# Short attention of a gated cross-attention block: row maxima as the bias of single exponentials, and a third buffer for context rows

## The reference, cut to what matters

```python
scores = einsum('bhqd,bhkd->bhqk', qh, kh) * inv_sqrt_d     # inv_sqrt_d = 1/sqrt(16)
scores = where(causal, scores, finfo(float32).min)
attn   = softmax(scores, axis=-1)
out    = einsum('bhqk,bhkd->bhqd', attn, vh)
# layers 1 to 3, ahead of their own attention over 1500 context rows of width 64:
kv_rope = kv_c * cos + rotate_half(kv_c) * sin
```

## Time and profile before

| | us |
|---|---|
| median of 3 runs | 2336.41 |
| lowest and highest run | 2328.46, 2338.89 |
| the profiled execution, own time | 2332.07 |
| its span, first to last instruction | 2330.3 |
| PE busy in the span | 2184.0 (94%) |
| DVE, ACT, POOL busy | 1478.2, 924.0, 1095.6 |
| mean granted TensorE clock | 0.963 |

### The profile page before, as it was taken

One profiled execution on the slowest core, in us unless ns is written; L12 is line 12 of the kernel. 1 busy time (PEld: TensorE's weight loads), 2 busy tenths in 40 slices (PEclk: granted clock), 3 DMA queues, 4 the chain that ended last, 5 costly groups with the idle time before them and its releaser, 6 DMA issues. The chain is left out here.

```text
span 2330.3 us, 38656 instructions
## 1 busy us (share of the span) xinstructions
PE 2184.0 (94%) x13766; PEld 1556.0 (67%) x13766; DVE 1478.2 (63%) x2519; ACT 924.0 (40%) x1433; POOL 1095.6 (47%) x618
## 2 busy tenths in 40 slices
PE   6768999999999998999999999897999999998998
PEld 4447998666566657666655665797665665677997
DVE  2765444577777757787777775412777777744444
ACT  1442443434444442113444444112444444424443
POOL 0330332047777760564777777101177777722332
PEclk9878999999999999999999999899999999998999
DMA  4482732374555513226455461384845545304332
GB/s 83 130 256 82 225 117 81 108 182 100 132 122 112 127 30 127 60 79 148 104 123 131 103 135 31 110 336 188 240 106 131 110 113 133 74 6 118 113 114 83
DMA packets 122054, 285.59 MB, mean 123 GB/s; under 512 B 31355, under 2 KB 73903, under 8 KB 118172
## 3 DMA queue, kind: packets, MB, share of 16 engines
q1 hardware_dynamic: 121244, 281.95, 45.6%
q0 software_dynamic: 672, 1.84, 0.2%
HBM read 237.15 MB, written 46.41 MB: 122 GB/s over the span
## 5 line engine op out<-in xcount | busy, mean ns | idle before, releaser
L1275 DVE TENSOR_REDUCE keep_top<-banks 128x1 f32<-128x500 f32 x945 | 596.0, 675 | 218.4 <-PE banks L1182 218.3
L1352 ACT ACTIVATE att_ex<-banks 125x896 f32<-125x896 f32 x576 | 500.9, 918 | 231.7 <-PE banks L1175 231.5
L1208 PE MATMUL banks<-att_ex,att_v 125*64 125x448 f32 x2304 | 464.7, 545 | 0.0
L1407 POOL TENSOR_TENSOR att_acc<-att_acc,att_ex 125x896 f32<-125x896 f32 x186 | 391.9, 2107 | 67.3 <-ACT att_ex L1352 53.5
L1407 POOL TENSOR_TENSOR att_acc<-att_acc,att_two 125x896 f32<-125x896 f32 x141 | 297.6, 2110 | 165.0 <-DVE att_two L1291 165.0
L1182 PE MATMUL banks<-keep_kh,keep_qt 64*128 64x500 f32 x1230 | 369.4, 406 | 2.8 <-POOL keep_eye L1390 2.8
L1208 PEld LDWEIGHTS banks<-att_ex,att_v 125*64 125x64 f32 x2304 | 152.5, 136 | 247.9 <-issue 209.3
L1175 PE MATMUL banks<-keep_qt,keep_kh 64*125 64x448 f32 x1152 | 308.8, 403 | 7.9 <-ACT att_ex L1352 2.7
L1175 PE MATMUL banks<-keep_qt,att_kl 64*125 64x448 f32 x1152 | 307.2, 363 | 0.0
L1722 PE MATMUL banks<-moe_xs,moe_w 128*128 128x448 f32 x1272 | 283.9, 373 | 4.0 <-DVE moe_w L1818 2.4
L1291 DVE TENSOR_TENSOR att_two<-att_ex 125x896 f32<-125x896 f32 x144 | 244.4, 1697 | 62.2 <-ACT att_ex L1352 59.5
(11 more groups left out here) (274 smaller groups left out, 2687.5 us busy)
## 6 DMA issues: line engine op xcount, KB each, us to landing
keep_kh<-kvt_hi SPq DMA_DIRECT2D x96, 375.0 KB, 5.2
att_kl<-kvt_lo SPq DMA_DIRECT2D x96, 375.0 KB, 7.2
q_rows<-mats_q SPq DMA_DIRECT2D x24, 896.0 KB, 4.8
keep_qt<-q_rows SPq DMA_DIRECT2D x96, 224.0 KB, 6.0
moe_raw<-L_experts_dram SPq DMA_DIRECT2D x53, 384.0 KB, 4.3
att_v<-kvn SPq DMA_DIRECT2D x24, 720.0 KB
sort_wu<-L_experts_dram SPq DMA_DIRECT2D x14, 1024.0 KB, 9.9
moe_cb<-comb_rows SPq DMA_DIRECT2D x62, 224.0 KB
```

Of the source, the lines that this page charges most:

```text
L1208: last = pe.matmul(PS[WEIGHED][64 * e:64 * e + 64, 0:HALF], v[:, s // 2, u, s % 2, :], ex[:, u % RING, e, :], start=u == 0, stop=u == UNIT ...
L1275: dve.tensor_reduce(top[:, s % 2, n // NS, n % NS:n % NS + 1], PS[MAXIMA + n % 3][:, 0:SB], AX.X, ALU.max).then_inc(mx_done, 1)
L1352: act.activation(ex[:, u % RING], scored, ACT.Exp).then_inc(exp_done, 1)
L1407: pool.tensor_tensor(a, a if n else ex[:, 0], two[:, i] if k == 2 else ex[:, k], ALU.add).then_inc(gathered, 1)
```

## The change

`Rotation` gets a third buffer of `cn`, loaded ahead like the first two (SP loads three pairs in an earlier stage, and pair m+1 instead of pair m in turn m of this stage), and a second buffer of `cm`, a tile of its own. POOL takes the sines of pair m+1 ahead of the sums of pair m; their wait is on the sums of pair m-1. DVE takes the cosines ahead of the two lows.

In `attend_short` DVE no longer subtracts the maxima from 448 or 336 columns; it multiplies the maxima with -SCALE into a small tile `nmx` (8 or 6 columns). DVE no longer sums the rows. ACT takes one exponential per tile of 128 rows and batch, 56 columns each, 14 for each pair, with `nmx` as the bias and `accum_out` for the sum of the row into `rs`. The semaphore `exp_done` goes up at the last of 8 and at the last of 6. DVE's inverses wait on it.

```diff
--- before.py
+++ after.py
@@ -180,14 +180,15 @@
     def __init__(self, G, keep):
         self.G = G
         self.cosN, self.sinN = keep.sb("cosN", [KP, NC * D]), keep.sb("sinN", [KP, NC * D])
-        self.cn = keep.sb("cn", [KP, 2, 2, NC * D])
-        self.cm = G["xn"][0:KP].rearrange("p t h -> p (t h)")[:, 0:2 * NC * D].rearrange("p (b n) -> p b n", b=2)
+        self.cn = keep.sb("cn", [KP, 3, 2, NC * D])
+        early = G["xn"][0:KP].rearrange("p t h -> p (t h)")[:, 0:2 * NC * D].rearrange("p (b n) -> p b n", b=2)
+        self.cm = [early, keep.sb("cm", [KP, 2, NC * D])]
         self.out_n, self.out_t = G["kvn_out"], G["kvt_out"]
 
     def start(self, st):
         self.cr = st.sb("cr", [KP, NC, 2, D])
         self.hi, self.lo = st.sb("hi", [128, 2, L], F32R), st.sb("lo", [128, 2, L], F32R)
-        self.in_n = [st.sem(f"in_n{u}") for u in range(2)]
+        self.in_n = [st.sem(f"in_n{u}") for u in range(3)]
         self.sin_n, self.cos_n, self.sum_n, self.turned, self.hi_t, self.lo_t = (
             st.sem(n) for n in ("sin_n", "cos_n", "sum_n", "turned", "hi_t", "lo_t"))
 
@@ -196,7 +197,7 @@
         for dst, src in ((self.cosN, "cosN"), (self.sinN, "sinN")):
             for a, z in self.ROWS:
                 yield dst[a:z, :], self.G[src][a:z, :]
-        for m in range(2):
+        for m in range(3):
             for a, z in self.ROWS:
                 yield self.cn[a:z, m], self.pair(m, a, z)
 
@@ -204,9 +205,9 @@
         return self.G["ctxN"][2 * m:2 * m + 2, a:z].rearrange("b p n -> p b n")
 
     def load(self, sp, m):
-        sp.wait_ge(self.sum_n, 2 * m - 2)
+        sp.wait_ge(self.sum_n, 2 * m - 4)
         for a, z in self.ROWS:
-            sp.dma_start(self.cn[a:z, m % 2], self.pair(m, a, z)).then_inc(self.in_n[m % 2], 16)
+            sp.dma_start(self.cn[a:z, m % 3], self.pair(m, a, z)).then_inc(self.in_n[m % 3], 16)
 
     def store_values(self, sp, m):
         sp.wait_ge(self.sum_n, 2 * m + 2)
@@ -220,17 +221,17 @@
         sp.dma_start(self.G["kvt_lo"][rows, :], self.lo[:, u, :].bitcast(FP32)).then_inc(self.out_t[u], 16)
 
     def sines(self, pool, m):
+        if m >= 3:
+            pool.wait_ge(self.in_n[m % 3], m // 3 * 32)
         if m >= 2:
-            pool.wait_ge(self.in_n[m % 2], m // 2 * 32)
-        if m:
-            pool.wait_ge(self.sum_n, 2 * m)
-        pool.tensor_tensor(self.cm[:], self.cn[:, m % 2],
+            pool.wait_ge(self.sum_n, 2 * m - 2)
+        pool.tensor_tensor(self.cm[m % 2][:, :, :], self.cn[:, m % 3],
                            self.sinN[:, :].unsqueeze(1).broadcast_to([KP, 2, NC * D]),
                            ALU.mult).then_inc(self.sin_n, 1)
 
     def cosines(self, dve, m):
         dve.wait_ge(self.sin_n, m + 1)
-        dve.tensor_tensor(self.cn[:, m % 2], self.cn[:, m % 2],
+        dve.tensor_tensor(self.cn[:, m % 3], self.cn[:, m % 3],
                           self.cosN[:, :].unsqueeze(1).broadcast_to([KP, 2, NC * D]), ALU.mult).then_inc(self.cos_n, 1)
 
     def sums(self, eng, m, e):
@@ -239,7 +240,7 @@
         if m:
             eng.wait_ge(self.turned, 3 * m)
             eng.wait_ge(self.out_n, 32 * m)
-        cn, cm = (v.rearrange("p b (c e d) -> p c b e d", e=2, d=D // 2) for v in (self.cn[:, m % 2], self.cm[:]))
+        cn, cm = (v.rearrange("p b (c e d) -> p c b e d", e=2, d=D // 2) for v in (self.cn[:, m % 3], self.cm[m % 2]))
         cr = self.cr[:].rearrange("p c b (e d) -> p c b e d", e=2)
         eng.tensor_tensor(cr[:, :, :, e], cn[:, :, :, e], cm[:, :, :, 1 - e], ALU.add).then_inc(self.sum_n, 1)
 
@@ -848,11 +849,10 @@
     GROUPS = ((0, 4), (4, NT))
     with Stage(nc, "att0") as st:
         p, pT = st.sb("p", [128, NT, 2, 64]), st.sb("pT", [128, T])
-        mx, rs = st.sb("mx", [128, NT, 2]), st.sb("rs", [128, NT, 2])
+        mx, nmx, rs = st.sb("mx", [128, NT, 2]), st.sb("nmx", [128, NT, 2]), st.sb("rs", [128, NT, 2])
         rot.start(st)
-        padded, s_ready, masked, maxed, centred, exp_done, summed, inverted, scaled = (
-            st.sem(n) for n in ("padded", "s_ready", "masked", "maxed", "centred", "exp_done", "summed", "inverted",
-                                "scaled"))
+        padded, s_ready, masked, maxed, negated, exp_done, inverted, scaled = (
+            st.sem(n) for n in ("padded", "s_ready", "masked", "maxed", "negated", "exp_done", "inverted", "scaled"))
         t_ready, t_copied, o_ready, placed = (st.sem(n) for n in ("t_ready", "t_copied", "o_ready", "placed"))
 
         def scored(m, g):
@@ -870,8 +870,8 @@
             def _(sp):
                 Stage.semaphores.clear_earlier(sp)
                 for m in range(B // 2):
-                    if m >= 2:
-                        rot.load(sp, m)
+                    if 3 <= m + 1 <= LAST:
+                        rot.load(sp, m + 1)
                     if m:
                         rot.store_values(sp, m - 1)
                     if m >= 2:
@@ -938,21 +938,18 @@
                     for g, (a, z) in enumerate(GROUPS):
                         dve.wait_ge(masked, 2 * m + g + 1)
                         dve.tensor_reduce(mx[:, a:z, :], scored(m, g), AX.X, ALU.max).then_inc(maxed, 1)
-                    for g in range(2):
+                    for g, (a, z) in enumerate(GROUPS):
                         dve.wait_ge(maxed, 2 * m + g + 1)
-                        dve.tensor_tensor(scored(m, g), scored(m, g), of_rows(mx, g), ALU.subtract).then_inc(centred, 1)
+                        dve.tensor_scalar(nmx[:, a:z, :], mx[:, a:z, :], -SCALE, None, ALU.mult).then_inc(negated, 1)
+                    rot.cosines(dve, m)
                     if m:
                         rot.turned_lows(dve, m - 1, 0)
                         rot.turned_lows(dve, m - 1, 1)
-                    rot.cosines(dve, m)
                     if m == LAST:
                         rot.turned_lows(dve, m - 1, 2)
                         rot.sums(dve, m, 0)
                     for g, (a, z) in enumerate(GROUPS):
                         dve.wait_ge(exp_done, 2 * m + g + 1)
-                        dve.tensor_reduce(rs[:, a:z, :], scored(m, g), AX.X, ALU.add).then_inc(summed, 1)
-                    for g, (a, z) in enumerate(GROUPS):
-                        dve.wait_ge(summed, 2 * m + g + 1)
                         dve.reciprocal(rs[:, a:z, :], rs[:, a:z, :]).then_inc(inverted, 1)
                     if m:
                         dve.wait_ge(t_ready, 2 * m)
@@ -985,9 +982,14 @@
                     if m:
                         rot.turned_highs(act, m - 1, 0)
                         rot.turned_highs(act, m - 1, 1)
-                    for g in range(2):
-                        act.wait_ge(centred, 2 * m + g + 1)
-                        act.activation(scored(m, g), scored(m, g), ACT.Exp, scale=SCALE).then_inc(exp_done, 1)
+                    for g, (a, z) in enumerate(GROUPS):
+                        act.wait_ge(negated, 2 * m + g + 1)
+                        for t in range(a, z):
+                            for u in range(2):
+                                row = scored(m, g)[:, t - a, u, :]
+                                last = act.activation(row, row, ACT.Exp, bias=nmx[:, t, u:u + 1], scale=SCALE,
+                                                      accum_out=rs[:, t, u:u + 1])
+                        last.then_inc(exp_done, 1)
                     if m:
                         place(m - 1)
                         rot.turned_highs(act, m - 1, 2)
@@ -1005,8 +1007,10 @@
             def _(pool):
                 pool.memset(p[:, :, :, S:], 0.0).then_inc(padded, 1)
                 pool.wait_ge(G["ahead_in"], G["ahead_expected"])
+                rot.sines(pool, 0)
                 for m in range(B // 2):
-                    rot.sines(pool, m)
+                    if m < LAST:
+                        rot.sines(pool, m + 1)
                     rot.sums(pool, m, 1)
 
 
```

## The result

The changed kernel takes 2354.79 us (median of 6 runs, 2346.44 to 2360.05), the kernel before 2333.37 us in runs taken beside them (6 runs, 2327.93 to 2338.89). The ratio is 1.0093, its 95% interval 1.0075 to 1.011: slower by 21.7 us, 17.5 to 25.7. The profiled execution took 2360.05 us, 28.0 more than the one of before; it is the slowest of the six, so its span overstates the loss.

A forecast was written before the change was run, and what follows sets the result against it. A loop through ACT, DVE and PE was taken to set the stage's pace. Six rounds +12.7, start +1.3 and end +3.8 gave 112 t - 19.2, +17.8 us at 330 ns: 2350 us, range 2329 to 2364.

The forecast's parts named there:

- ring: In short attention: highs, exponentials, place, highs, `pT` on ACT, then PE, then highs again; 11.39 us each time before.
- t: Time from one new exponential to the next on ACT; bounded at 127 to 420 ns, taken as 330.
- three signs of being wrong: Exponentials starting less than 276 ns apart; `pT` still waiting for PE in each pair; time moving in another stage.
- The round: One turn of the ring: 8.88 + 14 t, 13.50 us at 330 ns; six rounds 81.0 instead of 68.33, +12.7.
- ACT becomes gapless from first highs to `pT`, and DVE is hidden: Per pair, ACT's 1.51 us idle ahead of `pT` goes; about 2.0 us through DVE and PE hides behind ACT's work.
- Start: Pair 0, up to `pT`: 14 t - 3.34, +1.3 us at 330 ns.
- End: Pair 7, first to third highs: 14 t - 0.79, +3.8 us at 330 ns.
- The gain of cosines sooner: With sines a pair ahead, DVE's cosines stop waiting for POOL (once 1.21 us); already counted in the new round.
- the higher price: Rival: sum and exponential don't overlap on ACT, t 420 ns, +27.8 us, 2360 us; chance 0.15.
- the cheap sum: Rival: t near 217 ns, +5.1 us, 2337 us; chance 0.29 together with full clock in all six `weigh`.
- faster: Rival: exponentials at 127 ns and full clock in every `weigh`, -15.7 us, 2316 us; chance 0.08.
- The contention: Rival: DVE's cosines slowed beside POOL's sines, 9.4 us over eight pairs, 2359 us if on the path; chance 0.04.

The follow-up runs named there:

- place_split: The changed kernel with two of the four copies of `place` moved from ACT to DVE, behind the lows; one profile only, 2348.93 us.
- soft_only: The kernel before with only the softmax part of the change; ratio 1.007 (1.0053 to 1.0087) to the kernel before.
- third_late: The changed kernel with the third pair's two loads issued one stage later, in the fold stage; ratio 1.0094 (1.0059 to 1.013).
- rot_only: The kernel before with only the rotation part: three buffers, three loads ahead, sines a pair ahead, cosines ahead of the lows; ratio 1.0017 (0.9994 to 1.004).
- before_all_later: The kernel before with context rows, tables and next weights all issued one stage later, in the fold stage; ratio 0.998 (0.997 to 0.999).

## Why the prediction was right, and where it was not

The forecast was +17.8 us against a measured 21.7 (17.5 to 25.7), by the mechanism it named: the new exponentials lengthen a ring through ACT and PE. That the number came so near is luck in part, since errors of several us stood against one another. With the measured t its sum gives +12.5, so 5.3 us of the forecast were a t taken too long. Against that it had at nothing the wait of the transposes for `place` (4.8 us in six rounds), a slower PE in the first rounds (1.6), the barrier behind the third load (3.9) and 1.1 us at the start of the stage; with these and the -0.2 above, 12.5 comes to the 23.7 us by which the stage ends later in the profile.

Two of the prediction's three signs of being wrong were met. `pT` still waits for PE in each pair, if only for 5.9 us in eight waits instead of 15.5; and 3.9 us moved ahead of the stage. The third was not met, if by little: 283 ns against a limit of 276. Of what else it said would be seen, ACT is busy for 26.5 us more instead of 30, the stage takes 119.8 us instead of 118, DVE does wait for the exponentials, but the transposes wait for ACT's `place` where it said DVE.

*The ring* was right but for one link: highs, exponentials, `place`, then PE's transposes (the third highs run beside them), `pT`, PE. `place_split` shortened it by what it took from ACT.

*t* was mis-sized: 283 ns, not 330. The form was right (an exponential and a read, the next one starting under it). The size should have been put together from additions of 90 ns, not from the 203 ns of an instruction alone: an instruction in a row overlaps with both its neighbours. By 112 t - 19.2 the true t gives +12.5.

*The round* was forecast at 13.50 us, and 8.88 + 14 t is 12.84 at the true t. It took 13.66 in `soft_only` and `third_late` and 13.9 on average in the changed kernel. A round of `third_late` (103.63 to 117.30) is 0.95 us for the highs, 3.96 for the exponentials, 3.54 from `place` to `pT` and 5.22 from `pT` to the next highs. The forecast's terms for the same are 0.95, 3.96 at the true t, 2.74 and 5.19, so one of them was wrong. The step that failed is "ACT becomes gapless from first highs to `pT`, and DVE is hidden". DVE is hidden, as said: it waits for the exponentials 18 us in all. But the transposes wait for `place`, a semaphore that stood in the code and was hidden before by a late `p`, and so `place` to `pT` takes 3.54 us, not 2.74.

The changed kernel's first rounds are longer still, 14.03, 14.28 and 13.94, and the last three come down to 13.69. The granted clock goes with this. It is read from the 1.07 us ahead of the next first highs, in which PE makes the transposes that the highs read: in the first and the sixth round of the changed kernel, then in the first of `third_late` (columns of the earlier trace rows, the clock third from the end):

```profile
106.34:107.41 1.07, 1.07 (x7) 1.07 (x6) 1.07 (x3) 0.00 (x0) 0.34 (x1) 0.50 1.06 284
175.76:176.83 1.07, 1.07 (x8) 0.91 (x7) 0.50 (x1) 0.00 (x1) 0.00 (x0) 0.72 1.02 273
```

```profile
102.56:103.63 1.07, 1.07 (x7) 0.79 (x6) 1.07 (x3) 0.00 (x1) 0.44 (x1) 0.72 1.00 262
```

Over the six rounds of the changed kernel it is 0.50, 0.50, 0.60, 0.67, 0.70, 0.72, and 0.72 or 0.73 in all of `third_late`. So PE stayed at the half clock longer behind `weigh` in the first rounds; why it did isn't shown.

*Start*: +1.7 instead of +1.3. At the true t it would be +0.6, and `soft_only` has +0.4. The 1.3 us more in the changed kernel are 0.9 up to `pT`, the held negations, and 0.4 from there to the highs, on PE. That each negation costs at most 170 ns was wrong beside POOL's sines.

*End*: +3.2 instead of +3.8; 14 x 0.283 - 0.79 is 3.17. Only t was off.

*"The third load ahead falls into a stage in which nobody needs it: nothing"* cost +3.9 us in the profile. Nobody waits for the data, but everybody waits for the barrier behind the issue. `rot_only` (late start with the load ahead) and `third_late` (start repaired without it) show it from both sides, and `before_all_later` shows that the same barrier could give up another 5 us.

*The gain of cosines sooner* was taken to be in the round already. In the changed kernel no cosines wait for POOL; `rot_only` shows that by itself it was given back, to cosines that wait for the sines.

*The rivals*: the higher price and the cheap sum are both excluded by the spacing, *faster* too: t is 283 and `weigh` stayed at 3.35 us, the half clock, in seven of eight pairs. The contention, at 0.04, is real as a mechanism and costs the changed kernel 0.9 us where 9.4 were priced.

## What to carry to other kernels

Splitting one instruction on the slowest part of a loop into many cost a slot for each here (97 ns), and the pointer bias and the sum each added another (91 and 93); count those slots before counting what the neighbour engine saves. When a wait is removed, look in the code for the next semaphore that the same instruction waits for, not only in the profile, where it is hidden. Transfers issued ahead of a barrier can hold the other engines there, whenever the data is needed.

## What the runs showed of the hardware

- An exponential's row sum shows as an instruction of its own (`ACTIVATION_READ_ACCUMULATOR`, mean 248 ns long), and takes 93 ns of the engine's time in a row; a pointer bias takes 91 ns. Without either, 14 exponentials of 128x56 start 97 ns apart, less than half the 217 ns of a single one.
- DVE instructions of two kinds were held until POOL's running instruction ended, for up to 3.2 us: the cosines with both inputs in SBUF, and a `TENSOR_SCALAR` of 8 columns from SBUF to SBUF. Reductions and additions out of PSUM beside the same sines kept their length (1.04 us for two maxima). POOL's sines were held in the same way by cosines that had started first (4.66 us instead of 3.43). The Trainium skill (SBUF — State Buffer, Who interferes with whom) says that the order of issue decides which of the two engines blocks on the ports that they share; the rows agree both ways.
- Issuing a transfer took SP 0.4 us in some places and up to 4.15 in others, behind six context loads; behind four it was up to 1.7. What the queue waited for there isn't shown; no run isolates it.
